# A two-layer graph attention kernel on one core: the block moves are issued between the stack copies on SyncE's queue

## What is computed

```python
a = einsum('bnhd,bmhd->bhnm', q, k) * 384**-0.5 + bias[:, None]   # layer 0: bias = adj + adj
a = where(all(a == 0, -1), -inf, a)
o = einsum('bhnm,bmhd->bnhd', nan_to_num(softmax(a)), v).reshape(B, N, 384)
x = x + o @ Wo.T + bo       # q, k, v come from h = relu(layernorm(x)), v with its own bias
```

## Time and profile before

| | |
|---|---|
| median of 3 runs | 1577.4 us (1576.16 to 1578.65) |
| the profiled execution | 1577.92 us, span of its instructions 1576.1 us |
| granted TensorE clock, mean | 0.992 |
| busy: PE / PEld / DVE / ACT / POOL | 97% / 90% / 87% / 86% / 83% of the span |
| share of the 16 DMA engines, all queues | q1 (SyncE's) 71.3% |
| transfers: stack copies / block moves | 768 of 192 KB / 1024 of 64 KB |

### The profile page before, as it was taken

One profiled execution on the slowest core, in us unless ns is written; L12 is line 12 of the kernel. 1 busy time (PEld: TensorE's weight loads), 2 busy tenths in 40 slices (PEclk: granted clock), 3 DMA queues, 4 the chain that ended last, 5 costly groups with the idle time before them and its releaser, 6 DMA issues.

```text
span 1576.1 us, 45924 instructions
## 1 busy us (share of the span) xinstructions
PE 1524.9 (97%) x13184; PEld 1410.8 (90%) x13184; DVE 1372.9 (87%) x5190; ACT 1361.3 (86%) x4297; POOL 1314.7 (83%) x1673
## 2 busy tenths in 40 slices
PE   5999999999999999999999999999999999999996
PEld 5899899999899989899998998998999998998995
DVE  5899888989898988899888898888899888988984
ACT  5899888889888988898988898888898888888985
POOL 3788788888888888888888888888888888888885
PEclk9999999999999999999999999999999999999998
DMA  8667677777677776777776776777767777767763
GB/s 243 140 155 170 161 173 158 164 174 168 154 173 161 163 172 162 171 163 166 169 171 161 173 160 163 176 160 163 182 153 168 172 166 166 177 153 174 168 137 97
DMA packets 132538, 260.22 MB, mean 165 GB/s; under 512 B 30400, under 2 KB 58560, under 8 KB 132288
## 3 DMA queue, kind: packets, MB, share of 16 engines
q1 hardware_dynamic: 132288, 257.28, 71.3%
HBM read 26.48 MB, written 12.58 MB: 25 GB/s over the span
## 4 chain that ended last, share of the span: by engine, by line
PE 62%; SPq 21%; DMA 8%; issue 3%; DVE 3%; ACT 2%; POOL 0%; ACTq 0%; POOLq 0%; DVEq 0%
PE misc_bank L711 17%; SPq L242 11%; PE misc_bank L758 10%; PE probT_bank L652 10%; SPq L232 9%; PE misc_bank L730 9%; PE score_bank L640 8%; DMA stack<-split_qk 7%; PE values_bank L660 4%; PE values_bank L669 2%; PE misc_bank L691 2%; PE values_bank L746 2%; DVE split_qk L512 1%; ACT split_qk L435 1%; ACT prob L389 1%
## 5 line engine op out<-in xcount | busy, mean ns | idle before, releaser
L389 ACT ACTIVATE prob<-neg,guard 128x256 f32<-128x256 f32 x1536 | 765.4, 510 | 52.8 <-DVE guard L535 52.2
L535 DVE CUSTOM_DVE_ANT_0 neg<-score_bank,bias 128x256 f32<-128x256 f32 x1536 | 570.7, 415 | 55.2 <-PE score_bank L640 50.6
L308 POOL TENSOR_TENSOR half<-neg 128x256 f32<-128x256 f32 x768 | 549.7, 736 | 24.4 <-DVE guard L535 5.7
L640 PE MATMUL score_bank<-stack 96*128 96x256 f32 x1536 | 333.1, 306 | 5.8 <-DMA stack<-split_qk 4.3
L389 ACT ACTIVATION_READ_ACCUMULATOR prob<-neg,guard 128x1 f32 x1536 | 308.3, 201 | 0.0
L401 ACT ACTIVATE probT<-probT_bank 128x512 f32<-128x512 f32 x512 | 295.3, 592 | 5.9 <-PE probT_bank L652 5.9
L652 PE MATMUL probT_bank<-identity,prob 128*128 128x128 f32 x2048 | 290.7, 274 | 1.2 <-ACT probT L401 1.2
L640 PEld LDWEIGHTS score_bank<-stack 96*128 96x128 f32 x1536 | 234.9, 191 | 33.9 <-issue 25.5
L313 POOL TENSOR_TENSOR half<-half 128x512 f32<-128x512 f32 x192 | 246.7, 1285 | 15.1
L652 PEld LDWEIGHTS probT_bank<-identity,prob 128*128 128x128 f32 x2048 | 238.4, 141 | 9.6 <-ACT prob L389 1.4
L435 ACT ACTIVATE split_qk<-misc_bank 128x512 fp32r<-128x512 f32 x192 | 113.4, 591 | 106.5 <-DMA stack<-split_qk 88.8
(11 more groups left out here) (92 smaller groups left out, 3956.3 us busy)
## 6 DMA issues: line engine op xcount, KB each, us to landing
stack<-split_qk SPq DMA_DIRECT2D x768, 192.0 KB, 3.7
moved<-blocks SPq DMA_DIRECT2D x1024, 64.0 KB, 2.0
rows<-x SPq DMA_DIRECT2D x32, 384.0 KB, 4.8
out<-rows SPq DMA_DIRECT2D x32, 384.0 KB, 4.7
bias<-adj SPq DMA_DIRECT2D x32, 256.0 KB, 4.4
neg<-w0q SPq DMA_DIRECT2D x1, 576.0 KB, 4.3
prob<-w0k SPq DMA_DIRECT2D x1, 576.0 KB, 7.2
probT<-w0v SPq DMA_DIRECT2D x1, 576.0 KB, 8.2
```

The costliest lines, as they stand in the source:

```text
L308: nc.gpsimd.tensor_tensor(half[:, step % GROUP, :, :], n[:, :, 0:N // 2], n[:, :, N // 2:N], ALU.add).then_inc(half_done, 1)
L389: nc.scalar.activation(prob[:, step % PROB, q, :], neg[:, step % NEG, q, :], ACT.Exp, scale=-1.0, bias=guard[step // GROUP][:, step % GROU ...
L535: nc.vector.tensor_tensor_reduce(out=neg[:, step % NEG, q, :], in0=score_bank[step % 2][:, q * N:(q + 1) * N], in1=bias[u.t % GRAPHS][:, q ...
L640: mm = nc.tensor.matmul(score_bank[step % 2][:, q * N:(q + 1) * N], stack[:, g, 0, c * N + q * P:c * N + (q + 1) * P], stack[:, g, 1, c * ...
```

## The change

On SyncE's queue a slot before runs: quadrant 3 of the stack, the loads, the block moves to quadrants 0, 3 and 2, the stack's quadrants 0 and 1, the moves to quadrant 1, the stack's quadrant 2, the store. Now it runs: the moves to quadrants 1 and 0 (with the load of `rows` between them), the stack's quadrant 0 with the four moves to quadrant 2 between and behind its three copies, its quadrant 1 with the four moves to quadrant 3 likewise, its quadrants 2 and 3, the load of `bias`, the store. The number and size of all transfers stay as they were; `load_bias` is called a slot earlier for the same graph. The tables of the other four engines are written anew as well. Most of what changes there is the point at which the table is cut into slots; what is left are exchanges of neighbouring stages.

The diff, with the tables of the other engines cut to the lines where neighbours change places:

```diff
--- before.py
+++ after.py
@@ -222,25 +222,37 @@
                                x[u.t].rearrange("(i p) c -> p i c", p=P)
                                ).then_inc(rows_loaded[u.t % GRAPHS], 16)
 
-            def move_blocks(u, to):
+            def blocks_ready(u):
 
                 if u.k == 0:
                     sync.wait_ge(vo_low_done, 2)
                 sync.wait_ge(heads_ready, u.before(1).count(PARTS, 1))
                 sync.wait_ge(blocks_done, u.count(MOVED, MOVED))
+
+            def move_block(to, of):
+                sync.dma_start(moved[to * HEAD:(to + 1) * HEAD, of, :, :],
+                               blocks[of * HEAD:(of + 1) * HEAD, to, :, :]).then_inc(blocks_moved[to], 16)
+
+            def move_blocks(u, to):
+                blocks_ready(u)
                 for of in range(QUADS):
-                    sync.dma_start(moved[to * HEAD:(to + 1) * HEAD, of, :, :],
-                                   blocks[of * HEAD:(of + 1) * HEAD, to, :, :]).then_inc(blocks_moved[to], 16)
+                    move_block(to, of)
 
             def stack_quadrant(u, g):
 
                 sync.wait_ge(qk_low_done, u.count(CH, CH))
 
                 sync.wait_ge(scores_done, u.before(1).count(HEADS, CH * (g + 1)))
+                to = g + 2 if g < 2 and u.k > 0 else None
+                if to is not None:
+                    blocks_ready(u.before(1))
                 quad = split_qk[g * HEAD:(g + 1) * HEAD, :, :].bitcast(F32)
                 for part, (q, k) in enumerate(((1, 2), (1, 3), (0, 2))):
                     sync.dma_start(stack[part * HEAD:(part + 1) * HEAD, g, :, :].bitcast(F32),
                                    quad[:, q:k + 1:k - q, :]).then_inc(stacked[g], 16)
+                    if to is not None:
+                        for of in ((0,), (1,), (2, 3))[part]:
+                            move_block(to, of)
 
             def store(u, _):
                 sync.wait_ge(result_done, u.count(TILES, TILES))
@@ -267,14 +279,16 @@
 
             def slot(attend, project, output, norm):
                 for stage, u, i in (
-                    (stack_quadrant, attend, 3), (load_rows, norm, 0), (load_bias, project, 0),
-                    (move_blocks, attend, 0), (move_blocks, attend, 3), (move_blocks, attend, 2),
-                    (stack_quadrant, project, 0), (stack_quadrant, project, 1), (move_blocks, attend, 1),
-                    (stack_quadrant, project, 2), (store, output, 0),
+                    (move_blocks, attend, 1), (load_rows, norm, 0), (move_blocks, attend, 0),
+                    (stack_quadrant, project, 0), (move_blocks, attend, 3), (move_blocks, attend, 2),
+                    (stack_quadrant, project, 1), (stack_quadrant, project, 2), (stack_quadrant, project, 3),
+                    (load_bias, norm, 0), (store, output, 0),
                 ):
                     if u is None or stage in (load_bias, load_rows) and (u.layer == 1 or u.k < 2):
                         continue
                     if stage == store and u.layer == 0:
+                        continue
+                    if stage == move_blocks and i >= 2 and u.k < UNITS - 1:
                         continue
                     stage(u, i)
 
@@ -455,14 +468,15 @@
...
-                    (exps, attend, 2), (exps, attend, 3), (copy_probT, output, 11), (copy_sharesT, output, 0),
...
-                    (copy_probT, attend, 4), (qk_high, project, 2), (copy_probT, attend, 5), (exps, attend, 8),
...
+                    (copy_sharesT, output, 0), (exps, attend, 0), (exps, attend, 1), (exps, attend, 2),
+                    (copy_probT, output, 10), (spread_shares, output, 1), (copy_probT, output, 11),
+                    (exps, attend, 3), (exps, attend, 4), (qk_high, project, 0), (exps, attend, 5),
+                    (qk_high, project, 1), (copy_sharesT, output, 1), (exps, attend, 6), (copy_probT, attend, 4),
+                    (qk_high, project, 2), (exps, attend, 7), (copy_probT, attend, 5), (exps, attend, 8),
...
@@ -606,17 +620,17 @@
...
-                    (find_share, output, 2), (negate_scores, attend, 2), (negate_scores, attend, 3),
-                    (turn_blocks, attend, 0), (turn_blocks, attend, 1), (negate_scores, attend, 4),
...
-                    (find_share, attend, 0), (negate_scores, attend, 8), (negate_scores, attend, 9),
-                    (qk_low, project, 2), (result, output, 0), (statistics, norm, 0), (negate_scores, attend, 10),
...
+                    (negate_scores, attend, 1), (negate_scores, attend, 2), (find_share, output, 2),
+                    (turn_blocks, attend, 0), (negate_scores, attend, 3), (negate_scores, attend, 4),
...
+                    (qk_low, project, 1), (find_share, attend, 0), (negate_scores, attend, 8), (qk_low, project, 2),
+                    (negate_scores, attend, 9), (result, output, 0), (negate_scores, attend, 10),
...
@@ -775,16 +789,17 @@
...
-                    (transpose_shares, output, 1), (project_queries, project, 2), (project_keys, project, 2),
...
-                    (transposes, attend, 9), (scores, project, 0), (transpose_rows, norm, 0),
...
-                    (project_queries, norm, 0), (scores, project, 3), (project_queries, norm, 1),
...
+                    (scores, attend, 3), (scores, attend, 4), (project_keys, project, 0),
+                    (project_queries, project, 1), (scores, attend, 5), (weigh_values, output, 0),
...
+                    (transpose_shares, output, 1), (project_queries, project, 2), (scores, attend, 8),
+                    (project_keys, project, 2), (transposes, attend, 5), (scores, attend, 9),
...
```

More of the change, by code:

```diff
@@ L356, in slot @@
                 for stage, u, i in (
[L357 to L362, removed]
+                    (add_rest, attend, 1), (add_output_bias, project, 0), (invert_deviation, norm, 0),
+                    (add_half, attend, 8), (add_half, attend, 9), (add_half, attend, 10), (add_half, attend, 11),
+                    (add_rest, attend, 2), (add_half, project, 0), (add_half, project, 1), (add_half, project, 2),
+                    (add_half, project, 3), (add_rest, project, 0), (add_half, project, 4), (split_heads, attend, 0),
+                    (add_half, project, 5), (split_heads, attend, 1), (add_half, project, 6), (add_half, project, 7),
                 ):
@@ L457, in slot @@
                 for stage, u, i in (
[L458 to L465 removed]
+                    (rows_high, project, 0), (rows_high, project, 1), (copy_probT, output, 9),
+                    (copy_sharesT, output, 0), (exps, attend, 0), (exps, attend, 1), (exps, attend, 2),
[3 more added lines that the diff above has]
+                    (qk_high, project, 2), (exps, attend, 7), (copy_probT, attend, 5), (exps, attend, 8),
+                    (exps, attend, 9), (copy_probT, attend, 6), (exps, attend, 10), (copy_probT, attend, 7),
+                    (spread_shares, attend, 0), (exps, attend, 11), (normalise, norm, 0), (normalise, norm, 1),
+                    (copy_probT, attend, 8),
                 ):
@@ L608, in slot @@
                 for stage, u, i in (
-                    (mean, project, 1), (negate_scores, output, 11), (add_value_bias, attend, 0),
-                    (shift_rows, project, 0), (add_value_bias, attend, 1), (negate_scores, attend, 0),
-                    (rows_low, project, 0), (rows_low, project, 1), (negate_scores, attend, 1),
-                    (find_share, output, 2), (negate_scores, attend, 2), (negate_scores, attend, 3),
-                    (turn_blocks, attend, 0), (turn_blocks, attend, 1), (negate_scores, attend, 4),
-                    (turn_blocks, attend, 2), (turn_blocks, attend, 3), (scale_heads, output, 0),
-                    (negate_scores, attend, 5), (qk_low, project, 0), (negate_scores, attend, 6),
-                    (negate_scores, attend, 7), (scale_heads, output, 1), (qk_low, project, 1),
-                    (find_share, attend, 0), (negate_scores, attend, 8), (negate_scores, attend, 9),
-                    (qk_low, project, 2), (result, output, 0), (statistics, norm, 0), (negate_scores, attend, 10),
-                    (find_share, attend, 1), (result, output, 1), (statistics, norm, 1), (mean, norm, 0),
+                    (negate_scores, attend, 1), (negate_scores, attend, 2), (find_share, output, 2),
+                    (turn_blocks, attend, 0), (negate_scores, attend, 3), (negate_scores, attend, 4),
+                    (turn_blocks, attend, 1), (turn_blocks, attend, 2), (turn_blocks, attend, 3),
+                    (scale_heads, output, 0), (negate_scores, attend, 5), (qk_low, project, 0),
+                    (negate_scores, attend, 6), (negate_scores, attend, 7), (scale_heads, output, 1),
+                    (qk_low, project, 1), (find_share, attend, 0), (negate_scores, attend, 8), (qk_low, project, 2),
+                    (negate_scores, attend, 9), (result, output, 0), (negate_scores, attend, 10),
```

(4 more changed lines are left out.)

14 lines of the change are left out of this document (7 added, 7 removed).

## The result

| | before | changed |
|---|---|---|
| median | 1577.16 us (6 runs, 1575.67 to 1578.65) | 1567.42 us (6 runs, 1563.53 to 1570.96) |
| ratio to before | | 0.9936, 95% interval 0.9918 to 0.9954 |
| the profiled execution, its span | 1577.92, 1576.1 us | 1566.52, 1563.7 us |

The change makes the kernel faster, by 9.7 us. The forecast was 27 us, 1550. The range held the time; the size was wrong by more than half.

The account below looks back on a forecast made before the run. TensorE's floor of 23.34 us a slot bounds it, then SyncE's late transfer queue. From 1577.9 us, 26 of 35.0 us excess, 1.3 in the last unit and 0.5 for the median come off: 1550; range 1541 to 1572.

Parts of the forecast that it names:

- What bounds the kernel, and the floor: TensorE, busy 97%, bounds the kernel, with a floor of 23.34 us a slot; SyncE's transfer queue is the second bound.
- the 35 us counted as excess: Time of the 61 middle slots above 61 times 23.34 us: 35.0 us, all that a better order could give there.
- When the first copy can go: On SyncE's queue the first stack copy goes at W + 9.0 instead of 10.3; W is the slot's `weigh_values` start.
- until quadrant 3 has landed: The slot's last stack copies release ScalarE at 853.3 to 853.9, against 854.4 needed; before, 1.4 us late.
- Quadrant 1: Its last stack copy, now twelfth issue, lands 0.5 to 1.7 us before TensorE's head 3 scores: no cost, thin cover.
- the late moves: Last moves to quadrants 2 and 3 land at 847.0 to 849.1; VectorE's next `turn_blocks` can start at 848.57.
- rival A: The wait moves to quadrant 1's stack copy; half the gain is lost, 1564 us; chance 0.18.
- C: Rival: late moves behind the copies hold VectorE's `turn_blocks`, making the kernel slower, 1594 us; chance 0.12.
- The quarter of the excess that was kept: For irregular issues, 9 us of the middle slots' 35.0 us excess was assumed to stay, leaving a gain of 26.
- The reserve of 0.5 to 1.1 us: How early the slot's last stack copy lands before it would make TensorE wait: 0.5 to 1.1 us.
- The store ahead of the last copy: In the last unit TensorE waits 1.67 us for a stack copy; without the store ahead, 1.3 us of it goes.
- a floor above 23.34: Sign of a wrong prediction: slots' floor above 23.34 us, meaning exchanges on other engines cost something taken as hidden.

Follow-up runs that it names:

- e9: e8 with a second move to quadrant 2 put ahead of the first stack copy; 1542.44 us, ratio 0.9774 to the kernel before.
- e3: The kernel before with only SyncE's part of the change; 1582.99 us, ratio 1.0046 to the kernel before.
- e5: The changed kernel with each output-bias addition on GpSimd cut into pieces, six of 128 columns instead of two of 384; 1558.18 us, ratio 0.9872.
- e8: e1 with one move to quadrant 2 put ahead of the first stack copy; 1544.51 us, ratio 0.9780 to the kernel before.
- e1: The changed kernel with GpSimd's table as before; 1555.11 us, ratio 0.9868 to the kernel before.
- e10: e8 with GpSimd's table as in the changed kernel; 1562.07 us, ratio 0.9899 to the kernel before.

## Why the prediction was wrong in size

- *What bounds the kernel, and the floor.* Right, up to 3 us: e9 reaches the floor in practice, and its 1542 is what the prediction gave as the lower end, 1541. But every second slot has a floor of 23.44, so the mean is 23.39, and of the 35 us counted as excess some 3 could not go.
- *When the first copy can go; until quadrant 3 has landed.* Right: W + 8.9 and W + 26.1. That it needs the exchange on VectorE and ScalarE was said; how much hangs on it was not: without it the queue's part costs 0.46% (e3). That a copy cannot overtake a move issued ahead of it is so in the traces before and after: no stack copy landed before any of the moves among the twelve transfers ahead of it (in e5 two did and in e8 one, by 0.5 us at most).
- *Quadrant 1 and the late moves* (rivals A and C). Both reserves held in the changed kernel; quadrant 1 landed at W + 19.5 by the median, inside the 18.7 to 19.9 forecast. By the page's part 5, `turn_blocks` waited 1.0 us in all for moved blocks, so C is refuted. A is real where the start is late (e3, 25 times in the middle); with the early start scores waited for a copy in the middle at most twice a kernel (e1, e5).
- *The step that failed* is the part of the change on GpSimd. The prediction went through SyncE, VectorE, ScalarE and TensorE and took GpSimd's exchange as free without a reason. No GpSimd work that somebody waited for got late by it: GpSimd still waits 1.26 us for the mean (1.31 before), and e5 has the same order without the loss. But `share` on VectorE runs beside `add_output_bias` and is held, so that `result` starts 0.34 us later in a chain that had no reserve: in the kernel before, `normalise` ended at 844.49, when TensorE had begun `transpose_rows` at 844.36. The price, of which the forecast had none: 0.7%, some 11 of the 17 us that are missing, by the changed kernel over e1; and 1.2%, some 18 us, by e10 over e8, where no late copies hide a part of it.
- *The quarter of the excess that was kept*, 9 us, was too small a term; this is the other part of the missing 17. With GpSimd's table as before (e1) 21 us are won by the ratio where 27 were forecast. In e1's profiled execution the 61 slots took 1440.3 us, 18.4 less than before where 26 were forecast: 3 us of the rest are the alternating floor, some 13 are stalls. The reserve of 0.5 to 1.1 us was set against the scatter of the issues. What used it up was the landing of the last copy, taken as 3.2 us behind its issue: it was 4.1 to 5.0 in front of the 12 stalls. In the changed kernel the seven slots of 24.0 us and more are behind a landing of 4.5 to 4.9 us as well, all others behind one of at most 3.9. e8 shows that 0.6 us more reserve takes most of the stalls away.
- *The store ahead of the last copy*, 1.3 us. TensorE's wait in the last unit fell only from 1.67 to 0.92 us. Beyond the 61 slots the profiled execution got shorter by 3.7 us in all (before 1576.1 - 1458.7, now 1563.7 - 1450.0); no run separates the rest of this, and its cause stays open.

So 1550 was within 7 us for the queue's part by itself, and missed the new floor. The prediction named that sign itself ("a floor above 23.34"). That the time still lies in the stated range is luck: the range reached to 1572 to take in rival A, and the time came to 1567 for another reason.

## What to carry to other kernels

When a table is rewritten, go through every engine's moves, also those that fill an idle gap: ask for each what runs *beside* it, not only what is queued behind it. A VectorE instruction with two inputs in SBUF can, even with 8 elements a partition, last as long as the GpSimd instruction beside it (0.98 us here beside one of 1.0); put long GpSimd instructions next to other work, or cut them. And an order of transfers is only good with a start time: check when its first one may go, and put what is ready ahead of it into the idle time.

## What the runs showed of the hardware

- A VectorE instruction of 8 elements a partition with two inputs in SBUF took 0.17 us with GpSimd idle and up to 1.06 us beside an addition of 384 columns; beside additions of 128 columns (0.47 us each) it took 0.31 on average and 0.50 at most.
- One issue of a transfer on SyncE's queue took mostly 0.51 to 0.64 us while moves and copies alternated; six copies in a row took 4.56, 0.76 each. The median landing of a stack copy fell from 3.7 to 3.0 us with moves between the copies, that of a move rose from 2.0 to 2.4.
- In the middle of the changed kernel 42 single issues took more than 1.3 us, the longest 2.2, without a reason that the profile shows; before there were 73, up to 2.1. Where they come from stays open.
- The last stack copy of a slot landed mostly 3.0 to 3.5 us after its issue had ended, but in 12 of 60 slots of e1 after 4.1 to 5.0. This too stays open.
